# Gram matrices two samples at a time, and one more table looked up by one-hot in two more steps of a DLRM tower kernel

## What is computed

```python
e = stack([tbl_f[ids[:, f]] for f in range(26)], axis=1)      # 2048 x 26 x 128
sd = einsum('bfd,bd->bf', e, dense)                           # 26 dots with the dense vector
ss = einsum('bfd,bgd->bfg', e, e)                             # 26 x 26 dots of the embeddings
z = concatenate([dense, sd, ss[:, iu, ju], dense], axis=1)    # 351 pairs in all
h = maximum(z @ W_top1 + b_top1, 0.0)                         # 512
h = maximum(h @ W_top2 + b_top2, 0.0)                         # 256
y = h @ W_top3                                                # 1
```

## Time and profile before

| | us |
|---|---|
| median of 3 runs | 368.81 (367.70 to 369.45) |
| profiled execution, its own time | 368.79 |
| its span, first to last instruction | 367.0 |
| PE / PEld / DVE / ACT / POOL busy | 343.3 / 313.3 / 230.8 / 188.7 / 255.6 |

### The profile page before, as it was taken

How to read it: one execution, slowest core, us unless ns; L and a number is a source line. 1 busy time by engine, 2 the same in 40 slices (tenths; PEclk the granted TensorE clock), 3 DMA queues, 4 the chain that set the end, 5 groups by cost and what they waited for, 6 DMA issues and landing times.

```text
span 367.0 us, 13714 instructions
## 1 busy us (share of the span) xinstructions
PE 343.3 (94%) x6224; PEld 313.3 (85%) x6224; DVE 230.8 (63%) x324; ACT 188.7 (51%) x283; POOL 255.6 (70%) x273
## 2 busy tenths in 40 slices
PE   1998878999999999999999999999999999999986
PEld 0897777988989898989989898898989889897876
DVE  5799988965839294783929486592938469342030
ACT  1179574553737265553737255362646347372633
POOL 5778777777777777777777777777777777777000
PEclk9999998999999999999999999999999999999999
DMA  7994254222212222212212222212222212212000
GB/s 203 266 233 102 53 172 138 61 53 52 73 54 54 59 66 55 58 53 57 68 54 59 55 67 59 54 52 60 65 54 60 54 52 73 54 53 59 7 5 2
DMA packets 11755, 26.84 MB, mean 73 GB/s; under 512 B 4652, under 2 KB 5804, under 8 KB 11570
## 3 DMA queue, kind: packets, MB, share of 16 engines
q0 software_dynamic: 8512, 17.45, 18.2%
q1 hardware_dynamic: 3186, 8.52, 8.2%
HBM read 25.95 MB, written 0.01 MB: 71 GB/s over the span
## 4 chain that ended last, share of the span: by engine, by line
PE 90%; issue 3%; DVE 2%; DMA 2%; ACT 2%; SPq 0%; DVEq 0%; ACTq 0%
PE sum_bank L599 37%; PE vec_bank L626 14%; PE work L651 10%; PE vec_bank L612 7%; PE work L660 7%; PE work L647 4%; PE sum_bank L595 4%; PE id_bank L573 2%; DMA w_all<-in_tbl 2%; PE work L640 2%; DVE late L363 1%; PE work L666 1%; PE work L736 1%; DVE onehot L353 1%; DVE late L369 1%
## 5 line engine op out<-in xcount | busy, mean ns | idle before, releaser
L318 POOL DMA_INDIRECT rows<-in_tbl,ids_all x266 | 254.8, 958 | 83.3 <-issue 78.6
L353 DVE TENSOR_TENSOR onehot<-id_bank,row_f 125x1024 fp32r<-125x1024 f32 x150 | 174.8, 1217 | 92.0 <-PE sum_bank L599 47.5
L599 PE MATMUL sum_bank<-onehot,parts 125*128 125x256 f32 x1152 | 167.5, 292 | 1.7 <-issue 1.7
L599 PEld LDWEIGHTS sum_bank<-onehot,parts 125*128 125x128 f32 x1152 | 150.6, 192 | 5.7 <-issue 2.3
L433 ACT COPY vecT<-vec_bank 128x512 f32<-128x512 f32 (+1 forms) x74 | 84.9, 1150 | 16.8 <-PE vec_bank L612 16.4
L425 ACT COPY vecT<-sum_bank 128x256 f32<-128x256 f32 x75 | 52.4, 699 | 44.8 <-PE sum_bank L599 28.4
L626 PEld LDWEIGHTS vec_bank<-vecT 128*26 128x26 f32 x4096 | 44.2, 103 | 20.1 <-issue 14.7
L626 PE MATMUL vec_bank<-vecT 128*26 128x26 f32 x4096 | 54.1, 192 | 7.4 <-issue 1.9
L457 ACT ACTIVATE late<-work,w_all 128x256 f32<-128x256 f32 (+1 forms) x50 | 22.8, 458 | 49.6 <-PE work L651 31.4
L442 ACT COPY late<-vec_bank 128x416 f32<-128x416 f32 x32 | 16.2, 506 | 58.6 <-PE vec_bank L626 58.6
L363 DVE STREAM_TRANSPOSE late<-late 128x832 f32<-128x832 f32 x16 | 29.3, 1830 | 25.5 <-ACT late L442 25.5
(11 more groups left out here) (40 smaller groups left out, 103.9 us busy)
## 6 DMA issues: line engine op xcount, KB each, us to landing
rows<-in_tbl,ids_all POOLq DMA_INDIRECT x266, 2.6
late<-in_tbl SPq DMA_DIRECT2D x7, 480.0 KB
w_all<-in_weights SPq DMA_DIRECT2D x1, 1571.0 KB, 7.0
w_all<-in_tbl SPq DMA_DIRECT2D x3, 480.0 KB
xT<-in_dense_t SPq DMA_DIRECT2D x8, 128.0 KB
vecT<-in_ids_t SPq DMA_DIRECT2D x1, 256.0 KB, 2.8
late<-in_weights SPq DMA_DIRECT2D x1, 256.0 KB, 7.5
ids_all<-in_ids SPq DMA_DIRECT2D x1, 208.0 KB, 2.5
```

The costliest lines, as they stand in the source:

```text
L318: nc.gpsimd.indirect_dma_start(rows[:, tile % TD, FG * j + n, :], None, tables[f], bass.IndirectOffsetOnAxis(ids_all[:, tile, f:f + 1], 0) ...
L353: nc.vector.tensor_tensor(onehot[:, use % RING, 0:width, :], bass.AP(got.tensor, got.offset, [got.ap[0], [0, width], [1, DS]]), bass.AP(nu ...
L599: last = nc.tensor.matmul(into_sum, parts[:, k, CH_AT[n] + c0 + c, :], hot, start=first and k == 0, stop=final and k == PARTS - 1)
```

## The change

The gram takes two samples to a matmul. A sample's vectors stand in `vecT` in a space of 32 columns (`SPAN`) instead of 27; the last five are set to zero once by DVE. The stationary operand is the 64 columns of two samples, the moving operand their 2 x 26 vectors, and the output 64 partitions by 52 columns, of which the two diagonal blocks are wanted. There are 64 matmuls in a tile, in two groups of 64 output partitions, filling a bank four times (`FILLS`) with 8 x 52 columns. A drain copies, for each fill, the columns of the first samples for all partitions, and then those of the second samples over partitions 32 to 63 and 96 to 127, which are two copies more; in the last tile DVE makes these. The host permutes the order of the ids accordingly, and `copy_x` writes each tile of the dense vectors in the same permuted order. `TEN_STEPS` becomes 3, 4, 5, 6, 7. The loaded ids get a buffer of their own instead of a part of `vecT`.

```diff
-TEN_STEPS = [3, 5, 7]
+TEN_STEPS = [3, 4, 5, 6, 7]
...
-    HALF = 16
+    FILLS = 4
+    FILL = 8
+    SPAN = 32
...
-        return sum(groups(n) + 2 for n in range(tile)) + j
+        return sum(groups(n) + FILLS for n in range(tile)) + j
...
+    def gram_end(tile):
+        return gram_at(tile, FILLS - 1) + 1
...
+        def dots_of(use, second):
+            bank = vec_bank[use % 2][:, 0:FILL * 2 * GC].rearrange("p (i m f) -> p m i f", m=2, f=GC)
+            return bank[:, second, :, :]
...
-        vecT = sb("vecT", [P, SLOTS, P, VECS])
+        vecT = sb("vecT", [P, SLOTS, P, SPAN])
...
+            nc.vector.memset(vecT[:, :, :, VECS:SPAN], 0.0).then_inc(pad_set, 1)
...
+            def copy_last_seconds():
+                for f in range(FILLS):
+                    use = gram_at(TILES - 1, f)
+                    dve.wait_ge(firsts_copied, FILLS * (TILES - 1) + f + 1)
+                    for q in (BL, 3 * BL):
+                        last = nc.vector.tensor_copy(dots[q:q + BL, f * FILL:(f + 1) * FILL, :],
+                                                     dots_of(use, 1)[q:q + BL])
+                    last.then_inc(vec_drained, 1)
...
-                nc.scalar.copy(step_vec(d, place(0)), xT[:, d % 2, :].rearrange("p (t s) -> p t s", t=TD)).then_inc(x_copied, 1)
+                for t in range(TD):
+                    into = vecT[:, slot(TD * d + t), :, place(0)]
+                    last = nc.scalar.copy(into.rearrange("k (g i m) -> k g i m", g=2, m=2),
+                                          xT[:, d % 2, t * P:(t + 1) * P].rearrange("k (g m i) -> k g i m", g=2, m=2))
+                last.then_inc(x_copied, 1)
...
-                act.wait_ge(vec_filled, use + 1)
-                nc.scalar.copy(dots[:, h * HALF:(h + 1) * HALF, :],
-                               vec_bank[use % 2][:, 0:HALF * GC].rearrange("p (i f) -> p i f", f=GC)
-                               ).then_inc(vec_drained, 1)
+                for f in fills:
+                    use = gram_at(tile, f)
+                    act.wait_ge(vec_filled, use + 1)
+                    nc.scalar.copy(dots[:, f * FILL:(f + 1) * FILL, :], dots_of(use, 0)).then_inc(firsts_copied, 1)
+                for f in fills if tile < TILES - 1 else ():
+                    use = gram_at(tile, f)
+                    act.wait_ge(firsts_copied, FILLS * tile + f + 1)
+                    for q in (BL, 3 * BL):
+                        last = nc.scalar.copy(dots[q:q + BL, f * FILL:(f + 1) * FILL, :], dots_of(use, 1)[q:q + BL])
+                    last.then_inc(vec_drained, 1)
...
-                free_vec(into)
-                for i in range(HALF):
-                    for j in range(4):
-                        s = BL * j + h * HALF + i
-                        last = nc.tensor.matmul(vec_bank[into % 2][BL * j:BL * j + GC, i * GC:(i + 1) * GC],
-                                                vecT[:, slot(tile), s, 0:GC], vecT[:, slot(tile), s, 1:VECS],
-                                                start=True, stop=True)
-                last.then_inc(vec_filled, 1)
+                for f in range(FILLS // 2 * h, FILLS // 2 * (h + 1)):
+                    into = gram_at(tile, f)
+                    free_vec(into)
+                    for i in range(FILL):
+                        for g in range(2):
+                            s = 2 * (BL * g + f * FILL + i)
+                            last = nc.tensor.matmul(
+                                vec_bank[into % 2][2 * BL * g:2 * BL * (g + 1), 2 * i * GC:2 * (i + 1) * GC],
+                                vecT[:, slot(tile), s:s + 2, :].rearrange("k s v -> k (s v)"),
+                                vecT[:, slot(tile), s:s + 2, 1:VECS], start=True, stop=True)
+                    last.then_inc(vec_filled, 1)
```

More of the change, by code:

```diff
@@ L119, in rows_at, with gram_at @@
     def rows_at(tile, j):
-        return sum(groups(n) + 2 for n in range(tile)) + j
-    def gram_at(tile, h):
-        return rows_at(tile, groups(tile)) + h
+        return sum(groups(n) + FILLS for n in range(tile)) + j
+    def gram_at(tile, f):
+        return rows_at(tile, groups(tile)) + f
+    def gram_end(tile):
+        return gram_at(tile, FILLS - 1) + 1
     def same_rows(tile, j):
@@ L169, in sem @@
             return ctx.enter_context(nc.semaphore(name))
+        def dots_of(use, second):
+            bank = vec_bank[use % 2][:, 0:FILL * 2 * GC].rearrange("p (i m f) -> p m i f", m=2, f=GC)
+            return bank[:, second, :, :]
         def step_vec(d, v):
             first, second = (vecT[:, slot(TD * d + t), :, v:v + 1] for t in range(TD))
-            return bass.AP(first.tensor, first.offset, [first.ap[0], [second.offset - first.offset, TD], [VECS, P]])
+            return bass.AP(first.tensor, first.offset, [first.ap[0], [second.offset - first.offset, TD], [SPAN, P]])
         ids_all = sb("ids_all", [P, TILES, FEATS], i32)
@@ L181, in build @@
         idsT = sb("idsT", [P, TWO * DS], fp32r)
-        ids_i = vecT[:, 0, 0:(TWO * DS + VECS - 1) // VECS, :].rearrange("k s v -> k (s v)")[:, 0:TWO * DS].bitcast(i32)
+        ids_i = sb("ids_i", [P, TWO * DS], i32)
         y_lines = sb("y_lines", [P, BL * TILES])
@@ L247, in build @@
         vec_filled, vec_drained = sem("vec_filled"), sem("vec_drained")
+        pad_set, firsts_copied = sem("pad_set"), sem("firsts_copied")
         work_filled, work_drained = sem("work_filled"), sem("work_drained")
@@ L261, in _ @@
             sp.dma_start(ids_all[:], ids_v).then_inc(ids_loaded, 16)
-            sp.dma_start(ids_i, ids_t).then_inc(ids_t_loaded, 16)
+            sp.dma_start(ids_i[:], ids_t).then_inc(ids_t_loaded, 16)
             def load_table(n, dst, loaded):
@@ L308, in _ @@
                     if tile >= TD and j == 0:
-                        pool.wait_ge(vec_filled, gram_at(tile - TD, 1) + 1)
+                        pool.wait_ge(vec_filled, gram_end(tile - TD))
                     if tile >= TD and j == SECOND_HALF_FROM:
@@ L357, in set_pack @@
                     ALU.is_equal).then_inc(pack_set, 1)
+            def copy_last_seconds():
[6 more added lines that the diff above has]
+                    last.then_inc(vec_drained, 1)
             def turn(tile):
-                dve.wait_ge(vec_drained, gram_at(tile, 1) + 1)
+                dve.wait_ge(vec_drained, gram_end(tile))
                 if tile:
@@ L376, in _ @@
             dve.wait_ge(ids_t_loaded, 16)
-            nc.vector.tensor_copy(idsT[:], ids_i).then_inc(ids_cast, 1)
+            nc.vector.tensor_copy(idsT[:], ids_i[:]).then_inc(ids_cast, 1)
             dve.wait_ge(row_f_set, len(heights))
@@ L391, in _ @@
                     if k == TURN_AFTER:
+                        if tile == TILES - 1:
+                            copy_last_seconds()
                         turn(tile)
@@ L416, in copy_x @@
                 if d:
-                    act.wait_ge(vec_filled, gram_at(TD * (d - 1), 1) + 1)
-                nc.scalar.copy(step_vec(d, place(0)), xT[:, d % 2, :].rearrange("p (t s) -> p t s", t=TD)).then_inc(x_copied, 1)
+                    act.wait_ge(vec_filled, gram_end(TD * (d - 1)))
+                for t in range(TD):
[3 more added lines that the diff above has]
+                last.then_inc(x_copied, 1)
             def drain_sum(d, q):
@@ L437, in drain_gram @@
             def drain_gram(tile, h):
-                use = gram_at(tile, h)
+                fills = range(FILLS // 2 * h, FILLS // 2 * (h + 1))
                 if h == 0 and tile:
                     act.wait_ge(tile_turned, tile)
-                act.wait_ge(vec_filled, use + 1)
-                nc.scalar.copy(dots[:, h * HALF:(h + 1) * HALF, :],
-                               vec_bank[use % 2][:, 0:HALF * GC].rearrange("p (i f) -> p i f", f=GC)
-                               ).then_inc(vec_drained, 1)
+                for f in fills:
[8 more added lines that the diff above has]
+                    last.then_inc(vec_drained, 1)
             def drain_pairs(tile):
@@ L616, in gram @@
             def gram(tile, h):
-                into = gram_at(tile, h)
                 if h == 0:
+                    if tile == 0:
+                        pe.wait_ge(pad_set, 1)
                     pe.wait_ge(sum_drained, sum_at(tile // TD + 1, 0))
@@ L801 @@
     dense, ids = np.asarray(inputs["r_dense_features"]), np.asarray(inputs["ids"])
+    ids = ids.reshape(2, 2, 32, TILES, FEATS).transpose(0, 2, 1, 3, 4).reshape(BATCH, FEATS)
     add("dense_t", dense.reshape(P, TILES, DIM).transpose(2, 1, 0).reshape(DIM, BATCH))
```

## The result

The change makes the kernel slower: median 379.18 us of 4 runs (378.07 to 380.46) against 368.25 of 4 (367.31 to 369.45), a ratio of 1.0277 with a 95% interval from 1.0244 to 1.0310. The forecast was 383 (367 to 391). The profiled execution took 379.43 us, with a span of 377.6. That is 10.6 us more span than before.

The account below looks back on a forecast made before the run. The prediction took the kernel to be bound by one long queue on PE (TensorE), with POOL close behind. It summed 368.8 + 9.0 + 0.5 - 1.0 + 3.9 + 1.3 + 0.8 = 383.3, said 383 us, range 367 to 391.

Parts of the forecast that it names:

- The gram: Gram matmuls on PE: weight load decides at 29 ns an instruction, a half gram 2.02 us against 1.74; +9.0 us in all.
- The form change of +0.5: PE, between the gram and matmuls of different width, seven times: about 0.15 us each, 0 to 1.0, taken as +0.5.
- Feature 0: PE in steps 4 and 6, a tenth table each: 2.1 us a step, less 0.2 for transposes, +3.9 us together.
- The -1.0 that I took for stalls gone: PE: 4096 fewer instructions mean fewer instruction fetches, so stalls may go; 0 to -3 us, taken as -1.0.
- The start: ACT on the chain at the start: 1.1 us late to a table's low half, x copy split in two; +1.3 us, 0 to +4.
- The end: Last tile: final gram drain becomes three copies plus a handshake, +0.8 us (0 to +2); its gram halves +0.8 and -0.2.
- The cover of the drains: ACT between gram halves: 1.66 us of drain work fits within over 2.25 us of other PE work, so 0 us.
- (a): Gram on PE: the moving stream decides, gram worth -2.2 to +0.6 us, sum 372 to 375; chance 0.23.
- (b): Gram on PE: instruction count decides at 13.6 ns each, PE drops 24 us, POOL takes over, 357 us; chance 0.11.
- (c): Gram on PE: two groups 64 columns wide don't overlap, half gram 3.84 us, about 440 us; chance 0.05.
- (d): ACT turns bound: vecT's 32-word step doubles the strided part of its writes, 395 to 410 us; chance 0.06.
- POOL: Gathers on POOL: still back to back and ahead of PE by more than before; four fewer, -5.0 us, not the bound.

Follow-up runs that it names:

- The run without seconds: Changed kernel without the copies of the second samples on ACT and DVE, their dots left out: 377.57 us, ratio 1.0225.
- the 32 by 32 run: Kernel before with vecT step 32 and each gram matmul 32 stationary by 32 moving columns instead of 26 by 26: 369.48 us, ratio 0.9997.

## Why the prediction was right, point by point

The sum forecast +14.5 us and +10.9 were measured; the direction and the mechanism held, and nearly every term was too large.

**The gram, forecast +9.0, +0.5 and -1.0: measured +7.2.** The step that carried it, that the longest of supply, stream and load decides and that this is the load at 29 ns, held: 29.2 between starts, and a half of 2.00 us where 2.02 was worked out. That it held to 0.2 ns is luck in part. The 58 ns of a group were put together from 56 of load and 2 for the swap; no row shows the 2, and the runs show 53.3 and 5, two errors that cancel. The 32 halves sum to 64.2 us against 57.0. The 9.0 was 1.8 too large: 0.5 because a half is 2.005 and not 2.02, and 1.3 because 1.74 us stood for a half of before, read from one window, while the mean of the first 30 is 1.785, since three contain longer gaps of 0.4 to 0.8 us. The form change of +0.5 is in these numbers: halves ahead of layer 3 took 1.62 to 1.81 before and 2.00 or 2.01 after. A single clean instance undercounts what a wavering pace costs on average.

**Feature 0, forecast +3.9: measured +3.5 to +4.0** alone, and in the windows, with the gram halves taken out, 43.99 - 8.00 = 35.99 against 41.04 - 6.92 = 34.12, +1.9 a step. In windows that had ten tables before too, the same difference is -0.1 to -0.2 us (35.99 against 43.28 - 7.14), so PE's queue outside the gram got a little shorter there; PE idled for 0.4 to 0.6 us in such a window before and for none after. The -1.0 that I took for stalls gone may be this.

**The start, forecast +1.3: measured below 1.** The gram of tile 0 starts 0.35 us earlier and that of tile 1 0.21 later than before, 0.56 between them. The two halves of tile 0 are 0.16 shorter than before, since one had held a gap of 0.8, so up to the gram of tile 1 the rest is +0.4. ACT's last cast of the start ended 0.9 us later relative to the first gram, where 1.1 was worked out, and DVE's one-hot behind it made PE wait for 0.75. The x copies took 0.46 each instead of the 0.5 taken. The start of the changed kernel on PE, DVE and ACT (timeline), answering to rows 9:

```profile
1.21 1.66 DVE L335 MEMSET vecT<- 128x1920 f32 x1 [1.21 <-PEq L828]
...
3.85 0.43 DVE L397 CAST idsT<-ids_i 128x512 fp32r<-128x512 int32 x1 [0.88 <-DMA ids_i<-in_ids_t]
...
52.04 1.19 PE L631 MATMUL sum_bank<-onehot,parts 125*128 125x256 f32 x8 [0.75 <-DVE onehot L364]
```

The memset took 1.66 us (1.6 was worked out) and hid in the wait for the ids.

**The end, forecast +0.8 for the drain and +0.6 for the halves: measured +0.8 in all.** From the first gram half of tile 15 to the end it is 377.6 - 358.75 = 18.85 us against 367.0 - 348.91 = 18.09. The halves are +0.6 of it, so the handshake costs about 0.2 and not 0.8. In the last tile, DVE's copies follow ACT's closely (timeline of ACT and DVE after):

```profile
363.97 0.33 ACT L470 COPY late<-vec_bank 128x208 f32<-128x208 f32 x1 [0.60 <-PE vec_bank L661]
364.33 0.76 DVE L375 COPY late<-vec_bank 32x208 f32<-32x208 f32 x2 [0.17 <-ACT late L470]
365.13 1.76 DVE L383 STREAM_TRANSPOSE late<-late 128x832 f32<-128x832 f32 x1
```

0.33 and 0.76 for one of 0.51 were seen rightly, and PE waits 1.3 us for the pairs of this tile where it waited 0.3. From the transpose on, the tail is then 0.5 us shorter than before (377.6 - 365.13 against 367.0 - 354.04), which I didn't follow further.

**The cover of the drains held.** In the middle PE never idles, ACT waits for PE and not the other way round (timeline of ACT in tile 8 after, answering to rows 8):

```profile
210.94 0.33 ACT L470 COPY late<-vec_bank 128x208 f32<-128x208 f32 x1 [0.55 <-PE vec_bank L661]
211.30 1.34 ACT L475 COPY late<-vec_bank 32x208 f32<-32x208 f32 x4
212.86 0.47 ACT L489 ACTIVATE late<-work,w_all 128x256 f32<-128x256 f32 x1 [0.21 <-PE work L687]
```

Even behind the first half ACT comes back in time with 0.21 us to spare. The run without seconds confirms it from the other side: the same 43.99 us.

**The rivals.** (a) fell by the run with 58 columns and by that with 64 moving ones. (b), the count of instructions decides, fits the kernel before (the 32 by 32 run), if as a mean over gaps, and not the change; the 44 ns of stream that spoke against it were the right argument, and the load was stricter still. (c) fell: pairs of instructions in the two groups start within some 7 ns of each other. (d) fell with the wrong sign: a step of 32 words is cheaper to write, not dearer, which is most of why ACT's busy time is 223 us and not the 235 forecast (10 us less in the run with the step alone).

**POOL** didn't stay back to back, as I had said it would. It ran ahead until it had to wait for the gram (waits of POOL after):

```profile
POOL rows L328 <- issue: 76.2, 250, 0.3
POOL rows L328 <- PE vec_bank L661: 14.5, 6, 4.6
```

With 16 gathers in a tile it needs 20 us where PE takes 22, so the lead grows up to the permit of line 309, and then it waits. This costs nothing; I had left that permit out of the statement.

Of 10.6 us of span: +7.2 gram halves, +3.7 feature 0 (2 x 1.87), +0.4 start, +0.2 end, and a remainder of -0.9 outside the gram in the middle.

## What to carry to other kernels

Fewer instructions help only down to the next limit: before batching small matmuls, set the pace that the supply gives (here 13.9 ns an instruction on average over the gram, gaps included) beside what one batched instruction costs its column group, here the weight load plus about 5 ns, divided by the number of groups that still run side by side. Padding in the stationary operand is not free when the load is the longer one: six columns that nothing used were 4.4 us here. And work that one engine is to take over from another is worth its price only if the other one is the bound, which POOL wasn't.

## What the runs showed of the hardware

- In a column group, with a load at least as long as the stream, an fp32 matmul instruction's period is the load (0.83 ns a column) plus 5 ns: 58.4 ns at 64 stationary by 52 moving columns; halves of 2.00, 1.84 and 1.69 us at 64, 58 and 52 stationary columns. With 64 moving columns a half is 2.02. The load of the next runs beside the stream of this one, since 53.3 and 44 one after the other would be 97.
- In a long run of small matmuls (26 by 26, four column groups) starts are 9.2 ns apart, but twice in 128 instructions there is a gap of some 0.27 us: 16.7 us of 57.0 in all. With half the instructions there is none.
- Alternating between column groups of 64 and 32 puts 0.12 to 0.15 us between the last start of one width and the first of the other, at each change.
- ACT writing fp32 with a step of 32 words takes 1125 ns for 512 columns, with a step of 27 words 1252; 628 against 699 for 256. I had no row for it and have no explanation.
- Before and after the change PE idles for 2.6 us near 53 us, waiting for DVE, and in some executions the granted clock is at half, 1.2 GHz, for a while from then on (0.92 on average from 39.20 to 61.08 in the changed kernel, and 0.92 in the same stretch before), in others not (1.00 in the run without seconds, with the same wait). In the run with 58 columns one gram half fell into it, at a granted clock of 0.50, and took 3.38 us instead of 1.84; in that with 64 moving columns one took 3.57. The executions with 58 columns go from 372.68 us at a mean clock of 0.995 to 377.43 at 0.982, so a median of four or five can be off by 1 us or more for this alone.
